# A twelfth table looked up on TensorE, and the gathers' holds moved to the middle of the slot products

## What is computed

```python
combined = concatenate((dense[:, None, :], e), axis=1)      # 512 x 27 x 128
interactions = einsum('bfd,bgd->bfg', combined, combined)   # 27 x 27 per sample
z = concatenate((dense, interactions[:, iu, ju]), axis=1)   # the 351 pairs above the diagonal
h = concatenate([z, dense], axis=1)
h = maximum(h @ W_top1 + b_top1, 0.0)                       # 607 -> 512
h = maximum(h @ W_top2 + b_top2, 0.0)                       # 512 -> 256
y = h @ W_top3                                              # 256 -> 1
```

## Time and profile before

| | before |
|---|---|
| runs, median (lowest to highest) | 124.73 us (124.36 to 125.06) |
| span of the profiled execution | 123.0 us (its own device time isn't shown) |
| TensorE matmul, busy | 104.2 us, 85% |
| VectorE / ScalarE / GpSimd, busy | 65.4 / 48.1 / 65.7 us |
| mean granted TensorE clock | 0.902 |
| the chain that ended last | TensorE 83%, issue 13%, VectorE 2%, ScalarE 1% |

### The profile page before, as it was taken

One profiled execution on the slowest core, in us unless ns is written; L12 is line 12 of the kernel. 1 busy time (PEld: TensorE's weight loads), 2 busy tenths in 40 slices (PEclk: granted clock), 3 DMA queues, 4 the chain that ended last, 5 costly groups with the idle time before them and its releaser, 6 DMA issues.

```text
span 123.0 us, 3436 instructions
## 1 busy us (share of the span) xinstructions
PE 104.2 (85%) x1516; PEld 87.9 (71%) x1516; DVE 65.4 (53%) x110; ACT 48.1 (39%) x81; POOL 65.7 (53%) x66
## 2 busy tenths in 40 slices
PE   6999999999999999962178996289995299998993
PEld 6787888888888888831067895177992278996991
DVE  2599999999899996820001742105540106451411
ACT  4542979197794931300000462002541102730321
POOL 3887888579878887877500887503778305000000
PEclk9999999999999999999555999756999558999999
DMA  3799999999211112121200111200112100000000
GB/s 57 236 400 365 402 398 408 410 392 368 80 43 45 45 43 48 44 63 43 64 5 5 43 43 43 64 0 0 45 43 64 43 0 20 23 0 0 0 0 1
DMA packets 3949, 13.51 MB, mean 110 GB/s; under 512 B 1315, under 2 KB 1317, under 8 KB 3302
## 3 DMA queue, kind: packets, MB, share of 16 engines
q1 hardware_dynamic: 2018, 9.48, 20.5%
q0 software_dynamic: 1920, 3.94, 11.2%
q10 hardware_dynamic: 4, 0.00, 0.0%
HBM read 13.42 MB, written 0.00 MB: 109 GB/s over the span
## 4 chain that ended last, share of the span: by engine, by line
PE 83%; issue 13%; DVE 2%; ACT 1%
PE bank L365 17%; PE prod L408 13%; PE bank L414 13%; PE prod L365 12%; PE bank L374 7%; PE bank L504 6%; PE prod L433 4%; PE bank L321 4%; PE bank L325 3%; PE bank L445 2%; DVE inter_s L585 1%; PE bank L438 1%; PE prod L421 1%; PE bank L421 0%; DVE xT L575 0%
## 5 line engine op out<-in xcount | busy, mean ns | idle before, releaser
L313 POOL DMA_INDIRECT emb<-in_tbl,ids_sb x60 | 65.0, 1083 | 38.3 <-PE prod L408 19.3
L522 DVE TENSOR_SCALAR mask<-ids_h,ids_sb 128x1024 fp32r<-128x1024 int16 (+1 forms) x48 | 31.5, 699 | 2.2 <-issue 0.8
L408 PE MATMUL prod<-xT 128*27 128x27 f32 x1024 | 16.8, 215 | 14.7 <-issue 14.2
L408 PEld LDWEIGHTS prod<-xT 128*27 128x27 f32 x1024 | 13.6, 128 | 18.8 <-issue 17.4
L585 DVE STREAM_TRANSPOSE inter_s<-prod 128x288 f32<-128x288 f32 (+1 forms) x8 | 4.6, 611 | 26.3 <-PE prod L408 26.3
L365 PE MATMUL bank<-mask,high 128*128 128x512 f32 x46 | 15.2, 393 | 0.0
L365 PE MATMUL bank<-mask,low 128*128 128x512 f32 x46 | 15.0, 390 | 0.0
L414 PE MATMUL bank<-pairs,w_sb 117*128 117x128 f32 x96 | 12.7, 282 | 0.1
L414 PEld LDWEIGHTS bank<-pairs,w_sb 117*128 117x128 f32 x96 | 11.6, 191 | 0.7 <-ACT pairs L696 0.5
L531 DVE TENSOR_TENSOR low<-table,high 128x1024 fp32r<-128x1024 f32 (+1 forms) x9 | 11.7, 1301 | 0.0
L374 PE MATMUL bank<-ident,emb 128*128 128x128 f32 x60 | 10.5, 310 | 0.9 <-issue 0.9
(11 more groups left out here) (55 smaller groups left out, 118.1 us busy)
## 6 DMA issues: line engine op xcount, KB each, us to landing
table<-in_resident SPq DMA_DIRECT2D x3, 1024.0 KB
w_sb<-in_weights SPq DMA_DIRECT2D x1, 1792.0 KB
table<-in_resident SPq DMA_DIRECT2D x1, 1280.0 KB
table<-in_resident SPq DMA_DIRECT2D x4, 256.0 KB
emb<-in_tbl,ids_sb POOLq DMA_INDIRECT x60
ids_h<-in_other_ids SPq DMA_DIRECT2D x1, 896.0 KB
table<-in_resident SPq DMA_DIRECT2D x1, 640.0 KB
ids_h<-in_pair_ids SPq DMA_DIRECT2D x1, 256.0 KB
```

The source lines that it names most:

```text
L313: nc.gpsimd.indirect_dma_start(out=rows(t, c), out_offset=None, in_=gathered[c], in_offset=bass.IndirectOffsetOnAxis(ap=ids_sb[:, i:i + 1] ...
L408: mm = nc.tensor.matmul(prod[SLOT_PITCH * q:SLOT_PITCH * q + SLOTS, i, 0:SLOTS], x, x, start=True, stop=True)
L522: nc.vector.tensor_scalar(made(step)[:, 0:n, :], ids_h[:, 2 * b:2 * b + n, :], col_sb[:, row:row + 1], None, ALU.is_equal).then_inc(s_mask, 1)
```

## The change

Twelve tables are looked up and fourteen gathered, in groups of 4, 4, 3 and 3. Pair 5 has two tables of 1,250 rows; the second result uses the bank of turned group 1, so that pair waits for that group's packing. VectorE packs and keeps the results of both tables of pair 5. The nine holds of GpSimd become three, at the tenth gather of tile 3, the third of tile 4 and the tenth of tile 4. They wait for a new semaphore, `s_quiet`, which TensorE signals in each pass after 4 of the 16 groups of four calls in the second half of the products. TensorE's wait for `s_kept_last` moves ahead of the turning of group 1. ScalarE copies seven known slots a tile into place instead of six; VectorE's six are the same number.

```diff
-RESIDENT = 11
+RESIDENT = 12
-GROUPS = [(0, 4), (4, 4), (8, 4), (12, 3)]
+GROUPS = [(0, 4), (4, 4), (8, 3), (11, 3)]
+STIR = MATMULS // 2 + 4
-        look_banks = [l1_bank, half_bank, l1_bank, half_bank, l1_bank, [y_bank]]
+        look_banks = [l1_bank, half_bank, l1_bank, half_bank, l1_bank, [y_bank, t_bank[1]]]
+        s_quiet = sem("s_quiet")
             def hold(t, i):
-                if (t, i) == (1, 0):
-                    pool.wait_ge(s_used, first_step[2])
-                if (t, i) == (1, 8):
-                    pool.wait_ge(s_used, first_step[3] + 2)
-                if (t, i) == (2, 0):
-                    pool.wait_ge(s_used, first_step[4] + 3)
-                if (t, i) == (2, 6):
-                    pool.wait_ge(s_used, first_step[5] + 3)
-                if (t, i) == (2, 10):
-                    pool.wait_ge(s_prod, 1)
-                if (t, i) == (3, 0):
-                    pool.wait_ge(s_l1, 2)
-                if (t, i) == (3, 4):
-                    pool.wait_ge(s_prod, 2)
+                if (t, i) == (2, 9):
+                    pool.wait_ge(s_quiet, 1)
+                if (t, i) == (3, 2):
+                    pool.wait_ge(s_quiet, 2)
                 if (t, i) == (3, 9):
-                    pool.wait_ge(s_l1, 4)
-                if (t, i) == (3, 13):
-                    pool.wait_ge(s_prod, 3)
+                    pool.wait_ge(s_quiet, 3)
...
+                if b == len(PAIRS) - 1:
+                    pe.wait_ge(s_pack[1], 1)
                 look_up(b)
...
-                products(range(MATMULS // 2, MATMULS)).then_inc(s_prod, 1)
+                products(range(MATMULS // 2, STIR)).then_inc(s_quiet, 1)
+                products(range(STIR, MATMULS)).then_inc(s_prod, 1)
...
+                pe.wait_ge(s_kept_last, 1)
                 turn_next(p, (1,))
-                pe.wait_ge(s_kept_last, 1)
...
+            nc.vector.tensor_copy(*pack_looked(RESIDENT - 2))
             nc.vector.tensor_copy(*pack_looked(RESIDENT - 1)).then_inc(s_ready, 1)
+            nc.vector.tensor_copy(*keep_looked(RESIDENT - 2))
             nc.vector.tensor_copy(*keep_looked(RESIDENT - 1)).then_inc(s_kept_last, 1)
...
-                        dve.wait_ge(s_known, RESIDENT - 1)
+                        dve.wait_ge(s_known, RESIDENT - 2)
```

## The result

The changed kernel took 138.03 us (137.2 to 138.5, four runs) beside 124.9 for the kernel before: ratio 1.111, 95% interval 1.101 to 1.121. The time was forecast at 111.7, faster; it is slower. The span of the profiled execution grew from 123.0 to 136.4 us, with its device time at 138.5.

A forecast was written before the change was run, and what follows sets the result against it. Products were taken to crawl while gathers run, the clock falling after. Starts of products: +4.6 to tile 1, then -9.4, -5.2 and -3.0, together -13.0 from 124.73: 111.7 us, range 108.0 to 117.0.

The forecast's parts named there:

- Step (d): Seven gathers released at record 32 of tile 1's second half; tile 2's first half stalls 1.8 us, clock stays full.
- a slow clock only in products: Rival: clock falls in tiles 2 and 3's shorter stalls too, or gathers trail longer; 113.5 to 117 us, chance 0.22.
- (a): Lookups: the twelfth table's 20 added matmuls cost 4.54 us; first products start at 58.3 instead of 53.70.
- (b): Holds during lookups go: 37th gather starts at 55.9, flow free by 58.2 to 58.8, 0.2 us of stall.
- (c): Tile 1's products run free: 4.1 us from start to end, where they took 13.5.
- (e): Tile 3 goes as tile 2: first half ends at 85.85, products end at 87.8.
- (f): Last five gathers start after tile 3's signal; TensorE waits 1.5 us for the last; tile 4's products start at 97.1.
- The slower rival: Stalls in tiles 1 to 3 come from the loop's code fetch after the jump: 130.8 us, chance 0.06.
- the signs of being wrong: Tile 1's first half trickles with no gather in flight, clock keeps its dips, or tiles 2 and 3's hole stays as long.

The follow-up runs named there:

- r1: The changed kernel itself, timed again beside the kernel before in an even session: 111.4 us against 106.5, ratio 1.052.
- e8: Kernel before with twelve tables and its nine old holds (the table alone), even session: ratio 1.039.
- e9: Kernel before (eleven tables, nine holds) with its three holds on s_prod moved to the early signal, even session: ratio 1.004.
- e3: Kernel before with twelve tables and its nine old holds (the table alone), another even session: ratio 1.045.
- e4: Kernel before (eleven tables, nine holds) with its three holds on s_prod moved to the early signal, another even session: ratio 1.005.
- d2: Changed kernel with its three holds waiting for the end of the products, crawling session: two executions, 117.3 and 129.5 us, beside 125.1.
- u0: Kernel before with TensorE's loop over four tiles written out, no jump or branches, even session: 111.5 us against 107.0, ratio 1.040.
- d1: Kernel before (eleven tables) with its three holds on s_prod moved to the early signal, crawling session: 136.0 and 141.3 us beside 124.9.
- v1: Changed kernel with the signal 40 records before the products' end and gathers split 38, 7, 7, 4, crawling session: 131.98 us beside 125.3, ratio 1.050.
- e7: Changed kernel with its 19 late gathers replaced by same-size plain DMAs issued by GpSimd, crawling session: 127.8 us beside 125.3.

## Why the prediction was wrong

**Step (d) failed.** It took the gathers after the early signal as work behind the products, "0.95 us before its end", and let the 96 records left run out in those 0.95 us. They didn't: the crawl began 0.17 us after the first gather's start, with 44 records to go, and lasted for all seven gathers. The rule on which the forecast stands, that products crawl while gathers are under way, forbids that step. I had an end for the crawl, 2.25 to 2.85 us after the last gather's start, and never a beginning. The rows gave a hint of one: with gathers under way the products of tiles 1 to 3 stayed free for only 0.33 to 0.64 us (17 to 39 records). By the forecast's own end of a crawl the signal would have been priced so: from the first gather's start to 2.25 us after the seventh's, 6 x 1.25 + 2.25 = 9.75 us, in place of 0.95. It measured 9.9 in tile 1 (62.65 to 72.55), and the products took 12.2 us against 4.1, 11.9 against 5.0 and 10.3 against 5.0: together 20.4 of the 26.4 us between the span of 110.0 and 136.4. The early signal alone, +11.1 us on the kernel before, bears it out, and so does moving it to the end, which gave the forecast's timeline once (117.3), though not twice.

**The other 6 us.** 0.9 is the start: the first products began at 59.18, not 58.3, and in r1 with the same code at 57.85. 5.1 lie in the stretches behind the products (10.0, 10.1, 9.8 against 7.7, 7.7 and 9.3): in the first two, 2.0 us are still the end of the crawl, and behind it the clock is at 0.76 to 0.83. I had allowed for a slow clock only in products.

**(a)** The table's price was right on the whole: forecast +4.6 to the first product. In the sessions that have traces of both table counts, the first products come 3.7 to 5.1 us later with twelve (58.26 against 53.90 in e8 and e9, 58.75 against 54.10 in e3 and e4), and in even sessions the table alone costs 4.6 and 4.1 us.

**(b)** The 37th gather was forecast to start at 55.9 and started at 55.95, and tile 1's first half ran free. Right. **(c)** First half and gaps right, second half lost to (d). **(e)** fell with (d).

**(f)** No wait for the last gather in the changed kernel: the crawl delayed TensorE by more. Where the crawl was absent or short the wait was there, 1.16 us in r1 (forecast 1.5) and 2.4 in d2.

**The rivals.** None was this one. The slower rival had the stalls come from the loop and not from the gathers; they do go with gathers (no stall in tile 4, nor in any first half of the changed kernel). I had listed only ways in which the gathers' end is late, none in which their start is early. Of the signs of being wrong, one came true: the clock row kept its dips.

**The Trainium skill** (Runtime: NRT & Kernel Launch, Instruction fetch mechanics) was set against my reading with the jump back as the cause. The jump isn't it. In the kernel before tile 1 crawled without a jump. And TensorE's fetches are on record: queue q8 carries four packets in each of the two kernels, the last one started by 65.0 in the changed kernel and by 68.0 in the one before. The crawls of tiles 2 and 3 come later and see none. This is the table of queues of the kernel before from 74 to 82 us, in full; it has GpSimd's queue alone:

```profile
q0 software_dynamic: 162, 0.33, 15.0%
```

So no code is brought in behind any of the jumps back, and bringing in code isn't what makes tiles 2 and 3 crawl. The Trainium skill says in the same section that instructions come in 16 KiB blocks; u0 agrees (12 packets on q8 make 0.20 MB), and each of its four holes, of 1.2 to 2.5 us, begins within 2.1 us of the start of such a packet, so that there code to be brought in is the likely cause. The hole of tile 1 after 85 records is likely of the same kind, since q8 is silent after the first pass, and tiles 2 and 3 have no such hole. The free flow of all three tiles of the changed kernel ends after 84 records, but that needn't be a place in the code: the signal and with it the first gather's start, 0.17 us earlier, stand at a fixed record too. In d1 it is 84 again, 0.35 and 0.23 us after the gather's start.

**Open.** What makes a session crawling or even; what in an indirect gather slows the products, and why their free flow ends where it does; why the stretch behind the products crawls under gathers in v1 and in d1's tile 2 and neither in the kernel before nor in d2's first execution (in the two bad cases the first gather had begun 0.06 and 0.04 us before the products' end); and why d2 took 117 and 130. That gathers are needed for the crawl in crawling sessions rests on tile 4, on the first halves here, and on e7's plain DMAs, a single execution; the run without late gathers fell in even sessions both times.

No version tried is shown to beat the kernel before in both settings. In the one crawling session that has them, twelve tables with the old holds are 1.3% faster than before; in even sessions nothing is faster than the kernel before.

## What to carry to other kernels

When a release is moved ahead of a piece of work "because it hardly overlaps", price what is left of that piece at the rate that it has under the thing released, not at its free rate: 44 records of 0.01 us became 8.6 us. If two things can't overlap, an early signal can put the whole of the one into the other; a late one isn't free either: in even sessions the signal at the end took 113.2 and 114.3 us, the early one 111.4. And before a forecast rests on a stall with no releaser in the profile, time the unchanged kernel again in another session: a seventh of the time here (18 of 125 us) belonged to the setting.

## What the runs showed of the hardware

The same kernel takes 106.4 to 107.0 or 124.9 to 125.7 us, by the session. Under indirect gathers small matmuls slow in both, from 1.27 to 1.8 us for 128 records in even sessions and to some 5 records per 0.7 to 1.4 us in crawling ones; a crawl of the products ends 2.0 to 2.9 us after the last gather's start. Plain DMAs of the same size by SP (even session) or GpSimd (crawling session) and memsets (even session) don't do it, one execution each. In a crawling session other engines lose time too: VectorE started 2.8 us late in v1 and stood 6.3 and 4.9 us in e7. TensorE's loop of four passes brought in no code after its first pass, and none during the crawls of tiles 2 and 3. Written out, it took 12 blocks of code in place of 4 and 4% more time.
